# Three edits of a recommender kernel (CIN tower): the copy of e, the first base loads, the rounding of the dense inputs

## The reference

```python
e = jnp.stack([tbl_f[ids[:, f]] for f in range(39)], axis=1)
x = e
for W in (W0, W1):
    last = x.shape[1]
    inter = (x[:, :, None, :] * e[:, None, :, :]).reshape(B, last * F, D)
    x = jnp.einsum('bid,hi->bhd', inter, W)
    outs.append(x.sum(axis=-1))
z = jnp.concatenate(outs, axis=-1)
h = jnp.concatenate([z, dense_ctx], axis=1)
h = jnp.maximum(h @ W_top1 + b_top1, 0.0)
h = jnp.maximum(h @ W_top2 + b_top2, 0.0)
y = h @ W_top3
```

## Time and profile before

| what | value |
| --- | --- |
| time, median of 3 runs | 783.21 us (782.36 to 785.63) |
| the profiled execution's own time | 780.78 us |
| its span, first to last instruction | 779.0 us |
| mean granted TensorE clock | 0.991 |
| busy share of the span: TensorE matmul, weight load | 89%, 76% |
| VectorE, ScalarE, GpSimd | 87%, 54%, 64% |
| share of the span on the chain that ended last: TensorE, GpSimd, DMA, VectorE | 77%, 7%, 4%, 4% |

### The profile page before, as it was taken

The page is one execution under the profiler, slowest core; times in us unless marked ns, Lnnn a source line. Parts: engine busy times, 40 slices in busy tenths (PEclk is TensorE's granted clock), DMA queues, the critical chain, the costliest instruction groups (busy, mean ns, idle before and its releaser), DMA issues.

```text
span 779.0 us, 17028 instructions
## 1 busy us (share of the span) xinstructions
PE 696.8 (89%) x6210; PEld 595.1 (76%) x6210; DVE 674.9 (87%) x864; ACT 420.2 (54%) x769; POOL 501.0 (64%) x406
## 2 busy tenths in 40 slices
PE   0222678999999999999999999999999999999997
PEld 0222455878888888888888888888888888888887
DVE  5653999999999999999999999999999999888810
ACT  0001465656566656557565656655566656575741
POOL 6777887878787877868787887888787850000000
PEclk9999899999999999999999999999999999999999
DMA  4369569696867777787869796777867695854000
GB/s 101 90 156 275 129 184 164 164 171 170 163 167 168 131 185 130 187 134 190 161 163 168 173 162 169 171 148 182 141 171 142 162 160 138 162 153 133 13 7 1
DMA packets 171030, 115.67 MB, mean 148 GB/s; under 512 B 135043, under 2 KB 146906, under 8 KB 170563
## 3 DMA queue, kind: packets, MB, share of 16 engines
q1 hardware_dynamic: 154750, 108.80, 60.3%
q0 software_dynamic: 12800, 3.30, 6.6%
q10 hardware_dynamic: 3397, 2.47, 1.1%
HBM read 104.08 MB, written 15.53 MB: 154 GB/s over the span
## 4 chain that ended last, share of the span: by engine, by line
PE 77%; POOL 7%; DMA 4%; DVE 4%; issue 4%; SPq 3%; ACT 0%; DVEq 0%; ACTq 0%; POOLq 0%
PE z_ps L424 18%; PE x_ps L384 12%; PE x_ps L388 11%; PE x_ps L385 11%; PE g_ps L414 8%; POOL e_rows L360 7%; PE x1T_ps L445 4%; PE aux_ps L373 4%; PE x1T_ps L403 3%; PE x1T_ps L437 2%; SPq L280 2%; PE x1T_ps L435 2%; DVE product_lo L676 2%; DVE products L668 2%; DMA e_scratch<-e_d 2%
## 5 line engine op out<-in xcount | busy, mean ns | idle before, releaser
L360 POOL DMA_INDIRECT e_rows<-in_tbl_dram,ids_sb x400 | 500.6, 1252 | 134.7 <-issue 119.8
L514 ACT CAST product_hi<-products 117x1024 fp32r<-117x1024 f32 (+1 forms) x256 | 242.6, 948 | 102.7 <-DVE products L668 101.7
L676 DVE TENSOR_TENSOR product_lo<-products,product_hi 117x1024 fp32r<-117x1024 f32 (+1 forms) x256 | 277.4, 1084 | 23.1 <-ACT product_hi L514 22.9
L668 DVE TENSOR_TENSOR products<-bases 117x1024 f32<-117x1024 f32 (+1 forms) x256 | 277.5, 1084 | 7.1 <-DMA bases<-eT_scratch 6.5
L384 PE MATMUL x_ps<-product_hi,w_hi 117*128 117x512 f32 x448 | 198.5, 443 | 14.2 <-ACT product_hi L514 10.4
L424 PEld LDWEIGHTS z_ps<-G,w1T 128*128 128x128 f32 x1248 | 165.0, 191 | 17.3 <-issue 0.5
L385 PE MATMUL x_ps<-product_hi,w_lo 117*128 117x512 f32 x448 | 178.2, 398 | 0.0
L424 PE MATMUL z_ps<-G,w1T 128*128 128x128 f32 x1248 | 178.1, 280 | 0.0
L388 PE MATMUL x_ps<-product_lo,w_hi 117*128 117x512 f32 x448 | 148.5, 401 | 19.0 <-DVE product_lo L676 19.0
L388 PEld LDWEIGHTS x_ps<-product_lo,w_hi 117*128 117x128 f32 x448 | 84.3, 190 | 43.6 <-DVE product_lo L676 23.7
L384 PEld LDWEIGHTS x_ps<-product_hi,w_hi 117*128 117x128 f32 x448 | 85.6, 191 | 28.4 <-issue 13.8
(11 more groups left out here) (55 smaller groups left out, 340.1 us busy)
## 6 DMA issues: line engine op xcount, KB each, us to landing
bases<-eT_scratch SPq DMA_DIRECT2D x155, 468.0 KB
e_diag<-e_scratch SPq DMA_DIRECT2D x512, 10.0 KB
id_spread<-id_scratch SPq DMA_DIRECT2D x16, 437.5 KB
e_rows<-in_tbl_dram,ids_sb POOLq DMA_INDIRECT x400
e_scratch<-e_d SPq DMA_DIRECT2D x16, 320.0 KB, 9.5
eT_scratch<-e_rows SPq DMA_DIRECT2D x16, 312.0 KB
eT_scratch<-eT_scratch SPq DMA_DIRECT2D x16, 312.0 KB
w1T<-in_L_rec_W_dram SPq DMA_DIRECT2D x1, 2496.0 KB, 19.3
```

The source lines that it names most:

```text
L360: nc.gpsimd.indirect_dma_start(out=e_rows[t % E_SLOTS][:, f * D:(f + 1) * D], out_offset=None, in_=tables[f], in_offset=bass.IndirectOffse ...
L514: nc.scalar.copy(product_hi[:, first:first + count, :], products[:, first:first + count, :]).then_inc(hi_ready, 1)
L668: nc.vector.tensor_tensor(products[:, first:first + count, :], bases[u % 2][:, b:b + count, cols], bases[u % 2][:, a:a + 1, cols].to_broad ...
L676: nc.vector.tensor_tensor(product_lo[:, first:first + count, :], products[:, first:first + count, :], product_hi[:, first:first + count, : ...
```

## The change

Four things are done.

- `copy_e(t)` moves from VectorE to ScalarE. The copy of tile 0 stands ahead of ScalarE's wait for the doubled rows; the copy of tile t+1 stands at the end of chunk c == 2 of tile t, behind `round_products(g+1, 1)`, where on VectorE it stood in chunk c == 0.
- `store_e(t+1)` on SyncE moves from c == 0, behind `store_eT(t+1)`, to c == 3, behind `spread(g)` and ahead of the `load_bases` of the next chunk.
- The five DMAs of the first quarter are issued in turn by SyncE (bases 0, 2, 4) and ScalarE (1, 3). The second quarter is issued by SyncE after it has waited until the first has landed; everything that SyncE issues later stands behind that wait.
- The rounding of the dense inputs (`round_dense`, before L654) moves to ScalarE, for tiles 0 to 13 at c == 1 ahead of `round_products(g, 2)`, for the last two at the end of chunks 63 and 68. The remainder stays on VectorE.

```diff
-        def load_base_part(queue, t, first, count, ready):
+        def load_base_part(queue, t, first, count, ready, begin=0, step_of=1):
             at = first % HB * D
-            for a, starts in enumerate(BASES):
+            for a in range(begin, LOADS, step_of):
+                starts = BASES[a]
...
-            load_base_part(sp, 0, 0, HB // 2, first_ready[0])
+            load_base_part(sp, 0, 0, HB // 2, first_ready[0], 0, 2)
+            sp.wait_ge(first_ready[0], 16 * LOADS)
+            load_base_part(sp, 0, HB // 2, HB // 2, first_ready[1])
...
                 if c == 0 and t + 1 < TILES:
                     store_eT(t + 1)
+                if c == 3 and t + 1 < TILES:
                     store_e(t + 1)
...
+            def copy_e(t):
+                act.wait_ge(gathered[t % E_SLOTS], (t // E_SLOTS + 1) * 16 * len(GATHERED))
+                act.wait_ge(looked_up, (t + 1) * sum(map(len, SETS)))
+                after(act, e_stored, 16 * t)
+                nc.scalar.copy(e_d[:, :, 0:F], e_rows[t % E_SLOTS][:, :].rearrange("b (f d) -> b d f", d=D)).then_inc(e_d_ready, 1)
+
+            def round_dense(t):
+                act.wait_ge(dense_loaded, (t + 1) * 16 * 3 * GAP // D)
+                after(act, h1_in_ps, M1 * t)
+                nc.scalar.copy(dense_parts[:, :], dense_now[:, :]).then_inc(dense_hi_ready, 1)
...
+            copy_e(0)
             act.wait_ge(eT_doubled, 16)
-            load_base_part(act, 0, HB // 2, HB // 2, first_ready[1])
+            load_base_part(act, 0, 0, HB // 2, first_ready[0], 1, 2)
...
+                if c == 1 and 0 <= t - 2 < TILES - 2:
+                    round_dense(t - 2)
                 if g < CHUNKS:
                     round_products(g, 2)
...
                 if g + 1 < CHUNKS:
                     round_products(g + 1, 1)
+                if c == 2 and t + 1 < TILES:
+                    copy_e(t + 1)
+                if g == CHUNKS - 1:
+                    round_dense(TILES - 2)
+                if g == CHUNKS + CPT:
+                    round_dense(TILES - 1)
```

More of the change, by code:

```diff
@@ L607, in _ @@
         def _(dve):
-            def copy_e(t):
-                dve.wait_ge(gathered[t % E_SLOTS], (t // E_SLOTS + 1) * 16 * len(GATHERED))
-                dve.wait_ge(looked_up, (t + 1) * sum(map(len, SETS)))
-                after(dve, e_stored, 16 * t)
-                nc.vector.tensor_copy(e_d[:, :, 0:F], e_rows[t % E_SLOTS][:, :].rearrange("b (f d) -> b d f", d=D)).then_inc(e_d_ready, 1)
             def make_one_hot(t, n):
@@ L734, in _ @@
                                     wt1_dense[2 * GAP:3 * GAP, :].bitcast(f32), ALU.subtract).then_inc(wt1_dense_split, 1)
-            copy_e(0)
             make_k_mask(1)
@@ L753, in _ @@
                     pick_rows(t + 1, 3)
-                if c == 0 and t + 1 < TILES:
-                    copy_e(t + 1)
                 if c == 1 and t >= 2:
```

3 lines of the change are left out of this document (removed).

## The result

The changed kernel takes **794.78 us** (median of 4 runs, 792.35 to 797.81), the kernel before in the same session 783.17 us (4 runs). The ratio is 1.0145, 95% interval 1.0103 to 1.0186: slower by 1.5%, 11.6 us, where a gain of 5.0 was forecast. The profiled execution took 794.96 us, its span is 792.3 us.

What follows compares the result with a forecast made beforehand. TensorE was taken to bound the kernel from 200 us, VectorE the start-up. A 5.8 us start gain, six rounds costing 0.8 each and 3.9 of lead gave about -5: 783.2 - 5.0 = 778.2 us, range 772.8 to 784.5.

Steps and rivals of the forecast that it cites:

- Part 1, the first loads: Start-up: a quarter tile lands in 9.8 us, so first products start at 58.5 instead of 62.49 us.
- hidden by what follows: Chunk 1: the second quarter lands near 68.3, 1.7 us late, without effect because chunk 4 has to wait anyway.
- What is late next: Chunk 4: half tile 2 comes late through SyncE's order, so it starts at 104.7, 7.3 us earlier, not 15.8.
- the break: SyncE's queue at 58.5 us: its wait for the first quarter delays later bytes by 0.6 us, bounds 0 and 3.
- Tile 1: Half tiles 3 and 4: issued at 107.1 and 132.5, so chunk 8 starts at 146.8, 5.8 us earlier.
- The loop: SyncE's rounds: store_e ahead of a base load costs 0.8 us a round, 42.1 becoming 42.9, bounds 0.3 and 3.0.
- rival C: SyncE's loop: store_e's issue keeps its 1.85 us, a round costs 2.5 more, 788.5 us; chance 0.08.
- The loss stops there: SyncE's loop: from about 410 us on, after six rounds, its own waits take up the 0.8 us a round.
- The 23.4 us of waits: SyncE from about 410 us on: waits of its own, 23.4 us in all, which absorb the round's extra cost.
- the lead of 3.9 us: Loop: the loads' lead over TensorE, 3.1 us at chunk 11 and 3.9 six rounds on, is eaten before TensorE loses.
- ScalarE and GpSimd: The copy takes 0.7 us on ScalarE, hidden, as is the 0.3 us rounding; GpSimd's later gathers cost nothing.
- B: Rival: gain mostly lost, a round costing 1.3 us, 781.3 us, or the break 3 us; chance 0.28.

Runs made afterwards that it cites:

- e5: The changed kernel without SyncE's wait for the first quarter, the quarter still split over two sequencers: 788.97 us, ratio 1.0086.
- e1: The kernel before with only the new first base loads (split quarter and SyncE's wait): 789.29 us, ratio 1.0087.
- e10: The changed kernel with copy and store of e_d at c == 0 from tile 2 on, only tile 1's late: 791.06 us, ratio 1.0107.
- e2: The kernel before with only the copy of e on ScalarE at c == 2 and its store at c == 3: 782.59 us, ratio 1.0009.
- e7: e2 with ScalarE's copy at the end of c == 0 from tile 2 on, the store still at c == 3: 784.40 us, ratio 1.0028.
- e8: e7 with the store of e_d also back at c == 0 from tile 2 on: 780.06 us, ratio 0.9960.
- e3: The kernel before with only the rounding of the dense features moved to ScalarE: 781.88 us, ratio 0.9991.

## Why the prediction was wrong, point by point

**Part 1, the first loads: right.** First products at 59.41 (58.5 said). Without SyncE's wait (e5) they started at 60.91, near the 60.7 that two sequencers alone were to give. The second quarter landed 12.8 us after its issue at 59.41 where 9.8 was reckoned, and its 1.7 us of lateness "hidden by what follows" became a wait of 4.74 us in chunk 1; half tile 1 behind it was 1.37 us late for chunk 2. By themselves they did no harm, since chunk 4 had to wait another 10.01 us.

**"What is late next": this is the step that failed.** That SyncE would come to w1T near 71 was right (73.01). The sentence on it was "SyncE's queue carries the same bytes after as before, with one more break at 58.5. I take 0.6 us for the break (bounds 0 and 3)". The term measured 94.62 - 85.13 = 9.5 us. The queue carries the same bytes, but it carried them at full rate before: the earlier trace rows show 266 GB/s and a DMA share of 0.94 from 60 to 80 us. In a stretch at full rate there is nothing to catch up with. A break costs what the DMA engines could have moved in it, 2.58 MB, and the table above gives 3.1 to 4.2 us a MB in five kernels. The row stood in the prediction and was used for the size of a quarter, not for this. The bound of 3 us had no row under it.

From there the steps are right again with the 9 us put in: doubling to issue of half tile 2 5.0 us (4.7 said), issue to use 13.8 (14.3 said). Chunk 4 came at 113.45; 104.7 plus 8.9 is 113.6.

**Tile 1: a second term mis-sized.** From half tile 3 to half tile 4 25.4 us were reckoned, 0.4 of them for e_d's bytes; it was 146.49 - 116.93 = 29.6. The cost of `store_e(1)` at its new place is not its issue (0.54 us, as said) nor its bytes but who waits for it: the spreads of chunk 4, idle until 125.78, 3.2 us. The prediction named that wait for later tiles, as a small gain. With smaller entries (0.9 us in half tile 3's issue, 0.7 in half tile 4's way to its use) the 8.9 and 4.2 us make up the 14.7 between the 146.8 reckoned for chunk 8 and the 161.46 measured.

**The loop: mechanism right, price too small, end right.** 0.8 us a round was taken. From the doubling at 183.95 to the one at 317.09, three rounds, the changed kernel took 44.4 us a round, where the kernel before took 42.2 (174.93 to 301.62): 2.2 us a round, inside the bounds of 0.3 and 3.0 and close to rival C's 2.5. The mean from chunk 12 to chunk 56, (676.42 - 202.62) / 11 = 43.1 us a tile, looks like the 42.9 of the prediction, but it is 44.4 for three tiles and (676.42 - 335.71) / 8 = 42.6 after them. "The loss stops there" came true, by chunk 24 at 336 us and not at 410; why it stopped that early is not shown. The 23.4 us of waits that were to take it up are indeed used up. That is not due to the late start: e1 and e10, 4.9 and 10.8 us behind the kernel before at chunk 12, have their store of e_d at c == 0 and SyncE waits for TensorE 29.0 and 20.2 us in them from 200 to 700 us (us in total, times, longest):

```profile
SPq L72 <- PE g_ps L417: 29.0, 18, 2.7
...
SPq L72 <- PE g_ps L418: 20.2, 12, 2.8
```

With the store at c == 3 these waits are 1.0 us in e2 and none in e7 and in the changed kernel. That the place of `store_e` is the cause, and not the late gathers, is shown by e7 and e8. How much a round costs is not settled: from chunk 12 to chunk 56 e7 lost 8.0 us, the changed kernel 6.2, e2 0.5. The other part of the term was the lead of 3.9 us that the loads would have to eat first: behind the late start there was none, since VectorE waited for bases at chunk 12 already.

**ScalarE and GpSimd: right in the effect.** The copy took 1.29 us on ScalarE (median) and not 0.7, which cost nothing that the runs show. e3 shows the rounding hidden. GpSimd's gathers waited 49.5 us for the copy and it cost nothing (e7).

**Rival C, the only slower one, is refuted in its mechanism:** the issues of `store_e` took 0.42 to 0.54 us. B had the break at 3 us. No rival had the deferred bytes, though the same stretch row gives them.

The sum by parts: copy +0.8, loads +7.5, dense 0, together +8.3, for the whole +11.6. The rest is likely the copy's start-up gain, which is inside its +0.8 and which the loads take away.

**What stays open:** why the split moves fewer bytes early; why the loop's loss differs between kernels with the same place of the store; and why the 13.8 us between e8's and e10's chunk 12 (190.99 and 204.80) are more than e1's 4.9 over the kernel before; the order of waits in tile 1 differs in each, and no run separates them further. Part of it is that one execution stands for each: e1's profiled one took 785.84 us, 3.4 under its median, e10's 792.19, 1.1 over.

## What to carry to other kernels

Ahead of delaying any load, look at the GB/s of the stretch it is moved out of. If the DMA engines run at their full rate there, every byte that is put off arrives at the end of the stretch, for whoever stands last in it, at the full rate's price; making the first transfer faster by keeping the others back then only moves the wait. And a step that goes to another place in an in-order queue is priced by who waits for its result, not by its own issue.
